# Four graph-attention layers on 32 graphs: value products of two key blocks placed side by side on TensorE, one ring for masked scores and probabilities, a maxima pass that writes its own bank, and moved planned times

## The chip, the cores and the metric

One core of a Trainium2 chip runs the whole program; nothing is shared with other cores. The metric is the device time of one execution in microseconds (us). The kernel before took 2973.89 us in the median of 3 runs (2971.31 to 2974.82).

## What is computed

The input is 32 graphs of 512 nodes with 256 features each (float32) and one 512x512 adjacency matrix that all graphs share. Each graph goes through four residual layers with a layer norm behind each. All four are masked softmax attentions over the 512 nodes:

```python
# layer 0: one head, scores from two vectors
h = x @ W;  e = leaky_relu(s1[:, :, None] + s2[:, None, :]);  x = norm(x + elu(softmax(where(adj, e)) @ h))
# layer 1: eight heads of 32, scores q k^T, then a feed-forward block with two norms of its own
scores = einsum('fnhd,fmhd->fhnm', q, k) / sqrt(32);  attn = softmax(where(adj, scores));  t = attn @ v
# layer 2: four heads of 64, scores from two vectors per head, as layer 0
# layer 3: one head, e = leaky_relu((x W1) (x W2)^T);  x = norm(x + relu(softmax(where(adj, e)) @ (x W3)))
```

## The kernel before

A graph of 512 nodes is four blocks of 128 rows (NB = 4). Products run on PE (TensorE) mostly as float16 high and low parts, accumulated in the eight PSUM banks (`bank_ps`, 128x512 float32 each). Six graphs are in work at a time, in different layers, so that the engines always have something to do.

**The two ways of attention.** Layers 0, 2 and 3 work in units of one head and one block of 128 queries. ACT writes the leaky scores into a bank (`re`, L1115 and L1122; in layer 3 PE makes the scores first, `sc`, L1608). DVE adds the mask, negates and takes the row minimum (`mk`, L1334) into a buffer of the ring `masked` (4 entries). ACT takes the exponential (`ex`, L1133) from there into a buffer of the ring `prob` (7 entries). DVE makes the float16 high part and the row sum (`hi_v`, L1385), POOL the low part (`lo`, L910), a DMA transposes both (`tr`, L856), and PE multiplies them with the values (`pv`, L1627).

Layer 1 takes another way. PE makes the query-key products of four heads at once (`sq`, L1561, four banks), and DVE only needs the largest of each row of them (`mx`, L1349): the full result of that pass goes to a buffer `unused` that nobody reads, of two halves in turn, and each pass waits for the one two before it. The maxima are turned, stored as rows (`mh`, `mt`, `mr`, `md`) and added into the transposed scores. Those are made per pair of heads j (0 to 3), key block kb (0 to 3) and head e of the pair (0, 1): `u` (L1578 and L1579, two matmuls into one bank), ACT's exponential into a `prob` entry (`ue`, L1154), and then `pw` (L1587), once per j and kb: it multiplies the two heads' probabilities, in float32, with `value_ones`, into one accumulating bank (`acc1`), head 0 on its rows 0 to 63 and head 1 on rows 64 to 96. There are 32 x 4 x 4 = 512 `pw`. After kb = 3, `oc` (L1162) copies the bank and `bt` (L1597) turns it back.

**What sets the order.** A host-side planner, `schedule()`, plays the work through as a list schedule: each task has an engine, a planned duration (STEP), tasks that it comes after, ring entries that it opens and closes, and a due time (LEAD x graph + place in the graph's list + LATER of its kind). At each moment an idle engine takes the ready task with the earliest due time. The result is one fixed order for each of PE, ACT, DVE, POOL and SP (the queue that issues all DMAs), and for each ring entry the one who had it before (`prior`), which the code turns into semaphore waits. Each engine works strictly in its order. The `stack` task of SP (L825) is 12 DMA issues that copy q and k into the tensor `stack` of which there is only one: it waits for the last `u` of the graph before. PE's `job` tasks (L1525, L1532) are the dense layers; those of layer 2 (`h2`) wait for transposed rows that SP issues (`xd`, L844).

```python
                elif kind == "pw":
                    j, kb = key
                    pe.wait_ge(*dense_hi.last((g, "v", n) for n in range(2)))
                    bank = bank_of("acc1", g, j) if kb == 0 else bank_ps[entry("bank", "acc1", g, j)]
                    for e in range(2):
                        pe.wait_ge(*exp_done.at(g, j, kb, e))
```

## Time and profile before

| | |
|---|---|
| median of 3 runs | 2973.89 us (2971.31 to 2974.82) |
| the profiled execution: its time, its span | 2974.13 us, 2972.3 us |
| PE busy | 2773.1 us, 93% of the span |
| ACT busy | 2659.7 us, 89% |
| DVE busy | 2560.7 us, 86% |
| POOL busy | 2345.3 us, 79% |
| mean granted TensorE clock | 0.981 |

The time of an execution is its span plus about 2 us around it. Busy time of an engine is the union of its instructions' spans. A group of instructions is told as line, engine, operation, names, shapes and count, then its busy time, the mean duration of one in ns, and the engine's idle time just before them with what ended it. PEld is PE's weight load, which has rows of its own.

### The profile page before, as it was taken

What the parts mean: (1) busy time and instruction counts of PE and PEld (TensorE: products, weight loads), DVE (VectorE), ACT (ScalarE), POOL (GpSimd) and SP (SyncE); (2) the same over time, 40 slices, a digit from 0 to 9 for tenths busy, and PEclk for the clock granted to TensorE, in tenths of its full rate; (3) what the DMA queues carried; (4) which work ended last, traced back from release to release, by engine and by line L of the source; (5) the groups of instructions that cost most, each with busy time, mean ns of one, the idle gap of its engine ahead of it and who ended that gap; (6) DMA issues with size and microseconds to landing.
All of it is one profiled execution on the core that took longest, in us unless ns stands there. A gap on an engine that the chain in (4) does not pass through costs nothing. (4 is left out here: it accounts for less than half of the span.)

```text
span 2972.3 us, 69732 instructions
## 1 busy us (share of the span) xinstructions
PE 2773.1 (93%) x22576; PEld 1510.7 (51%) x22576; DVE 2560.7 (86%) x8261; ACT 2659.7 (89%) x5079; POOL 2345.3 (79%) x2517
## 2 busy tenths in 40 slices
PE   5999999999999999999999999999999999999855
PEld 4444445555555555545555554555555455554433
DVE  6778889889989888998989999898998889889764
ACT  6668889899999999999999999999989999898974
POOL 5467779788878888887888888788887888887774
PEclk9999999999999999999999999999999999999978
DMA  7355567767767767776676767677777777676565
GB/s 172 71 99 107 104 118 133 140 118 143 136 133 127 139 131 135 128 140 129 129 143 129 139 131 135 123 137 133 136 129 136 130 134 140 125 129 118 108 114 100
DMA packets 1215804, 378.91 MB, mean 127 GB/s; under 512 B 1157712, under 2 KB 1194320, under 8 KB 1215440
## 3 DMA queue, kind: packets, MB, share of 16 engines
q1 hardware_dynamic: 1213616, 373.46, 67.6%
q8 instruction: 180, 2.95, 0.4%
q10 hardware_dynamic: 1824, 0.99, 0.2%
q14 instruction: 184, 1.51, 0.2%
HBM read 21.43 MB, written 16.78 MB: 13 GB/s over the span
## 5 line engine op out<-in xcount | busy, mean ns | idle before, releaser
L910 POOL TENSOR_TENSOR split_r<-prob_r,split_r 128x512 f16<-128x512 f32 x768 | 880.5, 1159 | 275.8 <-DVE split_r L1385 272.9
L1349 DVE CUSTOM_DVE_ANT_0 unused<-bank_ps,neg_mask 128x512 bf16<-128x512 f32 x1024 | 661.7, 684 | 121.0 <-PE bank_ps L1561 120.3
L1627 PE MATMUL bank_ps<-val_r,trans_r 128*128 128x64 f16 (+1 forms) x9216 | 631.7, 222 | 72.9 <-DMA trans_r<-split_r 72.2
L1627 PEld LDWEIGHTS bank_ps<-val_r,trans_r 128*128 128x128 f16 x9216 | 526.9, 99 | 252.5 <-DMA trans_r<-split_r 74.8
L1154 ACT ACTIVATE prob_r<-bank_ps 128x512 f32<-128x512 f32 x1024 | 571.6, 607 | 48.7 <-PE bank_ps L1579 43.5
L1133 ACT ACTIVATE prob_r<-masked_r,low_r 128x512 f32<-128x512 f32 x768 | 535.8, 722 | 41.0 <-DVE low_r L1334 35.6
L1385 DVE TENSOR_SCALAR_CACHE_REDUCE split_r<-prob_r 128x512 f16<-128x512 f32 x768 | 510.9, 677 | 49.6 <-ACT prob_r L1133 25.7
L1587 PE MATMUL bank_ps<-prob_r,value_ones 128*33 128x512 f32 (+1 forms) x2048 | 546.1, 611 | 0.1
L1334 DVE CUSTOM_DVE_ANT_0 masked_r<-bank_ps,neg_mask 128x512 f32<-128x512 f32 x768 | 507.9, 683 | 31.0 <-ACT bank_ps L1122 22.9
L1578 PE MATMUL bank_ps<-stack 98*128 98x512 f16 x1024 | 393.3, 384 | 0.4 <-DVE low L1349 0.2
L1579 PE MATMUL bank_ps<-neg_mask_t,identb 128*128 128x512 bf16 x1024 | 389.6, 381 | 0.0
L891 POOL TENSOR_TENSOR split_r<-xcur,split_r 128x512 f16<-128x512 f32 x256 | 291.3, 1158 | 94.3 <-ACT split_r L1002 94.1
L1122 ACT ACTIVATE bank_ps<-spread_r,near 128x512 f32<-128x512 f32 x512 | 340.6, 699 | 14.3 <-DVE low L1349 8.8
L935 POOL TENSOR_TENSOR z<-z,xcur 128x512 f32<-128x512 f32 x192 | 241.7, 1272 | 97.9 <-DVE z L1373 44.0
L1532 PE MATMUL bank_ps<-w_h,xt_r 128*128 128x256 f16 x2304 | 283.0, 276 | 28.9 <-issue 14.7
L1435 DVE BATCH_NORM_STATS2 stats<-z 128x6 f32<-128x256 f32 x768 | 283.4, 415 | 26.1 <-POOL z L935 18.5
L1532 PEld LDWEIGHTS bank_ps<-w_h,xt_r 128*128 128x128 f16 x2304 | 224.4, 99 | 85.7 <-issue 30.0
L1578 PEld LDWEIGHTS bank_ps<-stack 98*128 98x128 f16 x1024 | 99.5, 97 | 275.3 <-issue 96.2
L1197 ACT ACTIVATE z<-z,offset,scale 128x256 f32<-128x256 f32 x384 | 203.4, 595 | 13.6 <-POOL offset L968 13.1
L965 POOL TENSOR_TENSOR scale<-scale,exponent 128x4 f32<-128x4 f32 x192 | 199.1, 1037 | 16.0
L1197 ACT ACTIVATE xcur<-z,offset,scale 128x256 f32<-128x256 f32 x384 | 207.8, 613 | 0.3 <-POOL offset L968 0.3
L1608 PE MATMUL bank_ps<-xt_r,proj_r 128*128 128x512 f16 x768 | 184.5, 382 | 0.0
(148 smaller groups left out, 4532.7 us busy)
## 6 DMA issues: line engine op xcount, KB each, us to landing
stack<-qk SPq DMA_DIRECT2D x384, 128.0 KB, 2.4
xcur<-in_x_dram SPq DMA_DIRECT2D x32, 512.0 KB, 4.0
out_dram<-z SPq DMA_DIRECT2D x32, 512.0 KB, 3.1
trans_r<-split_r SPq DMA_TRANSPOSE x768, 3.3
xt_r<-split_r SPq DMA_TRANSPOSE x320, 3.3
stack<-low_rows SPq DMA_DIRECT2D x128, 4.0 KB
qk<-in_adj_dram SPq DMA_DIRECT2D x1, 1024.0 KB, 7.9
z<-in_L_gnn_W_dram SPq DMA_DIRECT2D x4, 256.0 KB, 12.3
```

The lines of the kernel that those rows point to most:

```text
L910: nc.gpsimd.tensor_tensor(split_r[:, j, 1, :], prob_r[:, i, :], split_r[:, j, 0, :], ALU.subtract).then_inc(lo_done.sem, 1)
L1133: nc.scalar.activation(prob_r[:, entry("prob", *unit), :], masked_r[:, i, :], ACT.Exp, bias=low_r[:, i:i + 1], scale=-1.0).then_inc(probs_ ...
L1154: nc.scalar.activation(prob_r[:, entry("prob", "pt", g, *key), :], bank_ps[entry("bank", "u", g, *key)][:], ACT.Exp).then_inc(exp_done.sem, 1)
L1197: ins = nc.scalar.activation(dst[:, b, :], src[:, b, :], ACT.Identity, bias=offset[s][:, b:b + 1], scale=scale[s][:, b:b + 1])
L1334: nc.vector.tensor_tensor_reduce(out=masked_r[:, i, :], in0=bank_ps[entry("bank", "sc", *unit)][:], in1=neg_mask[:, b, :], scale=-1.0, sca ...
L1349: nc.vector.tensor_tensor_reduce(out=unused[:, nth % 2, :], in0=bank_ps[entry("bank", "sq", g, t, b, h)][:], in1=neg_mask[:, b, :], scale= ...
L1385: nc.vector.tensor_scalar(split_r[:, entry("split", *unit), 0, :], prob_r[:, entry("prob", *unit), :], 1.0, None, ALU.mult, ALU.add, accum ...
L1532: ins = nc.tensor.matmul(bank[:, half * C:(half + 1) * C], turned[:, t, xp, b * P:(b + 1) * P], W[job][:, wp, t, :], start=(i == 0), stop= ...
L1578: nc.tensor.matmul(bank[:], stack[:, h, 1, t, kb * P:(kb + 1) * P], stack[:, h, 0, t, :], start=True, stop=False)
L1579: nc.tensor.matmul(bank[:], identb[:], neg_mask_t[:, kb, :], start=False, stop=True).then_inc(turned_done.sem, 1)
L1587: ins = nc.tensor.matmul(bank[top:(64 if e == 0 else PAIR_COLS), :], value_ones[:, kb, j, cols], prob_r[:, entry("prob", "pt", g, j, kb, e ...
L1627: ins = nc.tensor.matmul(bank[:, at:at + width], trans_r[:, i, pp, jb, :], val(g, layer)[:, vp, jb, cols], start=(n == 0), stop=(n == len( ...
```

## The change

Five things change; what is computed stays the same.

1. `schedule()` runs as before, with the old ring sizes, but returns the planned start of each task. A new function `settle()` moves each planned start by NUDGE (per kind) and OFFSET (per place in the graph's list, 0 to 491), sorts each engine's tasks by the moved starts, and gives out all ring entries anew in that order.
2. For `pw`, the planned starts of kb 0 and 1 are both set to the later of the two, and so are those of kb 2 and 3 (PW_RUN = 2); the OFFSET of each is added behind that.
3. The rings `masked` and `prob` become one of 12 entries. `mk` writes into the entry, `ex` works in place in it. What `ex` waited for (the entry's former user) `mk` on DVE now waits for.
4. `mx` writes its full result into the bank that it reads, and its wait for the `mx` two before is gone; so is the buffer `unused`.
5. FIRST, LAST, SHIFT, LATER, STEP and the planner's rings stay as they are.

NUDGE has 105 entries from -3.4 to 6.8, OFFSET has 357; the places of `pw` in a graph's list are 136, 141, 146, 151 (j = 0), 160, 165, 170, 175 (j = 1), 184, 189, 194, 199 (j = 2) and 208, 213, 218, 223 (j = 3), and that of `stack` is 79. `pw` has no entry in NUDGE.

```diff
+    IN_RING = {"masked": "prob"}
+    RINGS = {**POOLS, "prob": 12}
...
+             "q_lo": 1.7, "rc_0": -0.9, "rc_2": -0.2, "rc_3": -0.6, "re_3": -0.9, "rp": 0.1, "rs_0": 2.9, "rs_1": 3.1, "rs_3":
+             4.9, "rs_ffn": -0.8, "rs_out": 0.1, "sc_3": 0.6, "shift": 2, "skip": 0.7, "spread_0": 0.3, "spread_2": 0.1, "sq":
+             -0.1, "st_0": -0.5, "st_2": 0.4, "st_3": 0.4, "st_out": 0.3, "stack": 6.8, "store": 1.2, "tr_0": -0.3, "tr_2": 0.2,
+             "tr_3": 0.2, "u": -0.2, "x_hi_0": 1.8, "x_hi_1": -1, "x_hi_2": -1.8, "x_hi_3": -1.3, "x_hi_ffn": -0.2, "x_lo_0":
...
+              0.5, 31: 0.2, 32: -0.1, 33: -1, 34: -0.4, 35: 0.7, 36: 1.3, 39: -0.4, 40: -1.4, 42: 1.6, 43: 0.5, 44: -0.3, 47:
...
+              -1.7, 66: 0.1, 67: 0.1, 69: 2.3, 70: -0.5, 71: 1.8, 72: -0.6, 74: -0.7, 75: 1.8, 76: 1.1, 77: -0.6, 79: 2.5, 81:
...
+              131: 2.8, 132: 0.3, 133: 0.1, 135: 1.1, 137: -1.1, 138: -1, 139: -1, 140: -0.9, 141: 0.2, 143: -0.2, 144: -0.4,
+              145: -0.1, 146: -1.5, 147: -0.6, 149: 0.5, 150: -0.2, 152: 0.4, 153: -0.1, 156: 0.2, 157: -0.2, 158: 0.4, 159:
+              0.1, 160: -0.3, 162: 0.6, 163: -0.5, 164: -0.4, 167: -0.7, 168: 2.2, 169: 2, 170: 0.1, 171: -1.2, 172: -1, 174:
+              0.1, 175: 0.1, 176: 0.8, 178: 0.3, 180: -0.1, 181: 1, 183: 0.6, 185: -2.2, 186: -0.5, 187: -0.6, 190: -0.1, 191:
+              1.6, 192: -2.2, 193: -2.2, 194: -0.5, 195: -2.1, 196: 0.5, 197: -2, 198: -0.4, 199: -0.5, 201: -0.5, 203: -0.4,
+              204: -0.1, 205: 0.4, 206: -0.5, 207: 0.5, 208: -0.2, 210: 0.4, 211: 0.5, 212: 0.8, 213: 0.1, 214: -0.4, 215: -0.3,
+              216: -0.5, 218: -0.1, 219: -0.4, 221: 0.8, 222: -0.2, 223: 0.4, 224: 0.8, 226: -0.4, 227: -1.3, 228: -1.1, 229:
...
+    DRIFT = {}
+    PW_RUN = 2
...
+    def settle(order, start):
...
+        for key, (_, us, _, _, closes, lands, (_, nth)) in tasks.items():
+            begin, ahead = start[key], 0.0
+            if key[0] == "pw" and PW_RUN > 1:
+                run = [(*key[:3], kb) for kb in range(key[3] // PW_RUN * PW_RUN, key[3] // PW_RUN * PW_RUN + PW_RUN)]
+                begin = max(start[k] for k in run)
+                ahead = 1e-4 * (tasks[run[-1]][6][1] - nth)
+            moved[key] = begin + NUDGE.get(kind_of(key), 0) + OFFSET.get(nth - first[key[1]], 0) + DRIFT.get(key[1], 0) - ahead
...
+        entries = {name: [[-1e18, None, n] for n in range(size)] for name, size in RINGS.items()}
+        in_turn = sorted(tasks, key=lambda key: (moved[key], tasks[key][6][1]))
+        for key in in_turn:
+            for name, opener in tasks[key][3]:
+                name = IN_RING.get(name, name)
+                if (name, opener) in place:
+                    continue
+                entry = min(entries[name], key=lambda e: (e[0], e[2]))
+                place[name, opener], before[name, opener] = entry[2], entry[1]
+                entry[0] = max(moved[k] + tasks[k][1] + tasks[k][5] for k in closers[name, opener])
+                entry[1] = opener
+        return {engine: [key for key in in_turn if tasks[key][0] == engine] for engine in order}, place, before
...
-        unused = sb("unused", [P, 2, N], bf16)
...
-        masked_r = sb("masked_r", [P, POOLS["masked"], N])
-        low_r = sb("low_r", [P, POOLS["masked"]])
-        prob_r = sb("prob_r", [P, POOLS["prob"], N])
+        low_r = sb("low_r", [P, RINGS["prob"]])
+        prob_r = sb("prob_r", [P, RINGS["prob"], N])
...
-                    was = prior("prob", *unit)
-                    if was is not None:
-                        act.wait_ge(*prob_free(was))
                     act.wait_ge(*masked_done.at(*unit))
-                    i = entry("masked", *unit)
-                    nc.scalar.activation(prob_r[:, entry("prob", *unit), :], masked_r[:, i, :], ACT.Exp,
+                    i = entry("prob", *unit)
+                    nc.scalar.activation(prob_r[:, i, :], prob_r[:, i, :], ACT.Exp,
...
-                        dve.wait_ge(*probs_done.at(*was))
+                        dve.wait_ge(*prob_free(was))
...
-                    nth = largest_done.at(g, t, b, h)[1]
-                    if nth > 2:
-                        dve.wait_ge(largest_done.sem, nth - 2)
+                    bank = bank_ps[entry("bank", "sq", g, t, b, h)][:]
                     eng.sem_inc(masking, 1)
-                    nc.vector.tensor_tensor_reduce(out=unused[:, nth % 2, :], in0=bank_ps[entry("bank", "sq", g, t, b, h)][:],
+                    nc.vector.tensor_tensor_reduce(out=bank, in0=bank,
```

## Rows read from the trace of the kernel before

**Rows 1.** The page: its span, and busy time of each engine.
```profile
span 2972.3 us, 69732 instructions
...
PE 2773.1 (93%) x22576; PEld 1510.7 (51%) x22576; DVE 2560.7 (86%) x8261; ACT 2659.7 (89%) x5079; POOL 2345.3 (79%) x2517
```

**Rows 2.** Busy time of each engine from 300 to 2800 us, with granted clock.
```profile
core 0: us, PE busy (x) PEld busy (x) DVE busy (x) ACT busy (x) POOL busy (x), PEclk, DMA share, GB/s
...
300.00:2800.00 2500.00, 2423.78 (x19886) 1311.54 (x19885) 2234.24 (x7265) 2336.19 (x4468) 2047.16 (x2195) 1.00 0.71 131
```

**Rows 3.** PE's own waits from 300 to 2760 us: total, times, longest.
```profile
PE bank_ps L1627 <- DMA trans_r<-split_r: 21.1, 32, 2.0
PE bank_ps L1532 <- issue: 14.7, 16, 2.4
PE bank_ps L1532 <- DMA xt_r<-split_r: 11.5, 7, 2.5
```

**Rows 4.** Timeline of PE around one pw that stands alone: start, duration, instruction.
```profile
1210.34 0.38 PE L1578 MATMUL bank_ps<-stack 98*128 98x512 f16 x1
1210.56 0.38 PE L1579 MATMUL bank_ps<-neg_mask_t,identb 128*128 128x512 bf16 x1
1210.87 1.07 PE L1587 MATMUL bank_ps<-prob_r,value_ones 128*64 128x512 f32 x4
1211.87 0.39 PE L1578 MATMUL bank_ps<-stack 98*128 98x512 f16 x1
```

**Rows 5.** Timeline of PE at the first and the last of 14 adjacent pairs.
```profile
578.15 0.38 PE L1579 MATMUL bank_ps<-neg_mask_t,identb 128*128 128x512 bf16 x1
578.46 1.93 PE L1587 MATMUL bank_ps<-prob_r,value_ones 128*64 128x512 f32 x8
...
2539.76 1.93 PE L1587 MATMUL bank_ps<-prob_r,value_ones 128*64 128x512 f32 x8
2541.62 0.55 PE L1627 MATMUL bank_ps<-val_r,trans_r 128*128 128x64 f16 x13
```

**Rows 6.** Timeline of PE's weight loads, around the lone pw and in a pair.
```profile
1210.34 0.10 PEld L1579 LDWEIGHTS bank_ps<-neg_mask_t,identb 128*128 128x128 bf16 x1
1210.86 0.19 PEld L1587 LDWEIGHTS bank_ps<-prob_r,value_ones 128*64 128x64 f32 x4 [0.43 <-issue]
1211.87 0.10 PEld L1578 LDWEIGHTS bank_ps<-stack 98*128 98x128 f16 x1 [0.81 <-DVE val_r L1310]
...
2540.65 0.16 PEld L1587 LDWEIGHTS bank_ps<-prob_r,value_ones 128*33 128x33 f32 x2 [0.27 <-issue]
```

**Rows 7.** Timeline of PE at the end of graph 14's layer-1 products, and 18 us on.
```profile
1225.04 1.07 PE L1587 MATMUL bank_ps<-prob_r,value_ones 128*64 128x512 f32 x4
1226.05 0.39 PE L1578 MATMUL bank_ps<-stack 98*128 98x512 f16 x1
...
1227.51 1.07 PE L1587 MATMUL bank_ps<-prob_r,value_ones 128*64 128x512 f32 x4
...
1244.67 1.58 PE L1532 MATMUL bank_ps<-w_h,xt_r 128*128 128x256 f16 x13 [1.12 <-DMA xt_r<-split_r]
```

**Rows 8.** Timeline of SP's DMA issues in the same stretch.
```profile
1226.68 7.93 SPq L825 DMA_DIRECT2D stack<-qk  x12
1234.75 4.06 SPq L856 DMA_TRANSPOSE trans_r<-split_r  x3
1238.93 2.66 SPq L844 DMA_TRANSPOSE xt_r<-split_r  x2
```

**Rows 9.** DVE's groups by shape: busy, mean ns, idle before and releaser.
```profile
L1349 DVE CUSTOM_DVE_ANT_0 unused<-bank_ps,neg_mask 128x512 bf16<-128x512 f32 x1024 | 661.7, 684 | 121.0 <-PE bank_ps L1561 120.3
L1399 DVE TENSOR_TENSOR bank_ps<-bank_ps,rinv 128x512 f32<-128x512 f32 x64 | 44.6, 697 | 1.5
```

**Rows 10.** Waits of ACT and DVE on ring entries: total, times, longest.
```profile
ACT prob_r L1133 <- POOL split_r L910: 4.6, 2, 4.2
...
DVE masked_r L1334 <- ACT prob_r L1133: 3.1, 1, 3.1
```

More of the change, by code:

```diff
@@ L122, in graph_layers_kernel @@
     SHIFT = {}
+    NUDGE = {"add_0": 0.7, "add_3": 2.4, "ap_0": -0.5, "ap_1": -0.6, "ap_2": -2.2, "ap_3": 1, "ap_ffn": -0.4, "ap_out": -0.1,
[13 rows of a table added]
+    OFFSET = {0: -5.3, 1: -2.7, 2: 2.5, 3: -0.3, 4: -0.4, 5: 2.3, 6: -0.3, 7: -0.1, 8: -0.1, 9: 0.2, 11: -0.2, 12: -0.6, 14:
[32 rows of a table added]
+    DRIFT = {}
+    PW_RUN = 2
     STEP = {"add_0": 1.22, "add_1": 1.23, "add_3": 1.23, "ap_0": 0.97, "ap_1": 0.99, "ap_2": 0.98, "ap_3": 0.98, "ap_ffn": 0.98,
@@ L369, in schedule @@
         open_entries = {}
+        start = {}
         now, left = 0.0, len(tasks)
@@ L404, in schedule @@
                 order[engine].append(best)
+                start[best] = now
                 end = now + us
@@ L433, in schedule, with kind_of @@
                 now = events[0]
-        return order, place, before, max(ends.values())
-    ORDER, PLACE, BEFORE, LENGTH = schedule()
+        return order, start, max(ends.values())
+    def settle(order, start):
+        def kind_of(key):
+            return f"{key[0]}_{key[2]}" if key[0] in BY_STAGE else key[0]
+        moved, closers = {}, {}
+        for key, (_, us, _, _, closes, lands, (_, nth)) in tasks.items():
[5 more added lines that the diff above has]
+            moved[key] = begin + NUDGE.get(kind_of(key), 0) + OFFSET.get(nth - first[key[1]], 0) + DRIFT.get(key[1], 0) - ahead
+            for name, opener in closes:
+                closers.setdefault((IN_RING.get(name, name), opener), []).append(key)
+        place, before = {}, {}
+        entries = {name: [[-1e18, None, n] for n in range(size)] for name, size in RINGS.items()}
[10 more added lines that the diff above has]
+        return {engine: [key for key in in_turn if tasks[key][0] == engine] for engine in order}, place, before
+    PLANNED, START, LENGTH = schedule()
+    ORDER, PLACE, BEFORE = settle(PLANNED, START)
     print("planned", LENGTH, {e: round(sum(tasks[k][1] for k in ORDER[e])) for e in ORDER})
@@ L1327, in _ @@
                     layer, h, b = key
-                    i = entry("masked", *unit)
-                    was = prior("masked", *unit)
+                    i = entry("prob", *unit)
+                    was = prior("prob", *unit)
                     if was is not None:
-                        dve.wait_ge(*probs_done.at(*was))
+                        dve.wait_ge(*prob_free(was))
                     dve.wait_ge(*leaky_done.at(*unit))
                     eng.sem_inc(masking, 1)
-                    nc.vector.tensor_tensor_reduce(out=masked_r[:, i, :], in0=bank_ps[entry("bank", "sc", *unit)][:],
+                    nc.vector.tensor_tensor_reduce(out=prob_r[:, i, :], in0=bank_ps[entry("bank", "sc", *unit)][:],
                                                    in1=neg_mask[:, b, :],
```

32 rows, old and new, of tables (NUDGE, OFFSET) are left out of this document.

## The prediction

> **What bounds the kernel now.** I read the page first [rows 1]: PE is busy 2773.1 us of a span of 2972.3 us, ACT 2659.7, DVE 2560.7. PE has the most work, but an average over the span does not say that it sets the pace, so the second view is busy time by stretch [rows 2]. From 300 to 2800 us, where the pipeline of graphs runs full, PE is busy 2423.78 of 2500 us, 97%, at a granted clock of 1.00; ACT is at 93%, DVE at 89%, POOL at 82%. There PE is the bound: it is idle for 76 us only, and a microsecond taken from PE's own work comes off the time unless a new wait replaces it. In the two ends together, 472 us, PE is busy for 2773 - 2424 = 349 us and idle for 123; they go by chains of waits, and I leave them at nothing. Third are PE's own waits in the full stretch [rows 3]: 21.1 us for transposed probabilities, and 14.7 + 11.5 = 26.2 us, in 23 waits, at L1532, where the dense layer of layer 2 waits for transposed rows (its "issue" rows stand at the same point of the cycle). Fourth is the timeline of PE at L1587, the instruction that the change moves most.
>
> **Part 1, pw in pairs.** What does one `pw` cost where it stands alone? A float16 matmul of 512 columns is followed by the next after 0.22 us (1210.34 to 1210.56), but 0.31 us pass before `pw` starts (1210.56 to 1210.87), so entering it costs 0.09 us; the next work starts 1.00 us after it (1211.87) [rows 4]. Together 1.09 us, and 2.18 for two. The trace of before already has 14 places where two `pw` happen to stand side by side; the first and the last show one block of eight matmuls of 1.93 us, and the next work starts 1.86 us after its beginning (2539.76 to 2541.62), with 0.31 us of lead again (578.15 to 578.46) [rows 5]. With the entry that is 1.95 us. A pair that comes to stand together saves 2.18 - 1.95 = 0.23 us. Why it does is seen in the weight loads: the load for a lone `pw` starts with it and the load of the work behind it starts only when that work does, after 0.81 us of idle load path, while in the pair of 2539.76 further loads lie under its running matmuls (2540.65) [rows 5, 6]. The pair pays entry and exit once.
>
> The Trainium skill (TensorE: Matmul & The Clock Gate, "What overlaps and what doesn't") says that a weight load overlaps running matmuls only when it goes to another row group. All loads of `pw` use all 128 rows, so by that rule the two would overlap nothing and pairing would give nothing: this part of the sum would be 0. The trace disagrees already in float16, where the load at 1210.34 runs beside a matmul on the same rows [rows 4, 6], and the pair's 1.95 us disagrees again.
>
> How many pairs form? There are 512 `pw`, so 256 runs of two. `settle` gives both the same start, but then adds OFFSET of each one's own place, and where the two differ something else can be sorted between. The differences are: places 141 and 136 0.2, 151 and 146 1.5, 165 and 160 0.3, 175 and 170 none, 189 and 184 none, 199 and 194 none, 213 and 208 0.3, 223 and 218 0.5. The plan of before starts 116 PE tasks per graph, one each 0.8 us, and most before a `pw` are 0.36 us or longer. Adding the diff's moves to the planned starts around them, by hand for graphs 14 and 15, seven of the eight runs stay together and kb 2 and 3 of j = 0 part. That is 7 x 32 = 224, of which 14 exist: 210 x 0.23 = **48 us** less PE work. Bounds: 242 x 0.23 = 56 us if all form, 6 x 32 = 192, less 14, so 178 x 0.23 = 41 us if one more per graph parts. The price of waiting is small: the pair starts where kb 1 or 3 stood, whose exponentials were done by then; kb 0's two entries of the ring are held one `pw` interval longer, some 2 us [rows 7].
>
> **Part 2, what moves past the last u.** PE's last `pw` of kb 2 stands in front of the last `u` of the graph (1225.04, then 1226.05), that of kb 3 behind it (1227.51) [rows 7]. As a pair both stand behind. SP's `stack` issues wait for that last `u`: they start at 1226.68, take 7.93 us, then three transposes and then the two of the rows that layer 2 needs, until 1241.6 [rows 8], and PE waits for these for 1.12 us at 1244.67 [rows 7]. With kb 2 behind the `u`, SP is let go 1.09 us earlier, while PE, with a pair in place of one `pw` behind the `u`, has 1.95 - 1.09 = 0.86 us more to do before it comes to L1532. So the wait should shrink by up to 0.86 us in each of 28 graphs, and the average of it is 26.2 / 28 = 0.94 us [rows 3]. I take **16 us**, two thirds of 24; bounds are nothing (SP is then held by the low parts of POOL instead) and the whole 26.
>
> One move looks as if it did the same and doesn't. `stack` is moved by 6.8 + 2.5 = 9.3 us later. But its planned duration is 9.6 us, so the next task of SP was planned 9.6 us behind it; 9.3 us later it still stands in front of it, and its 12 issues with it. SP's order is nearly that of before, and I count nothing.
>
> **Part 3, the shared ring.** An attention unit held one entry of 4 and then one of 7; now one of 12. The wait for the old user leaves ACT and goes to DVE. On ACT it ended idle time of 4.6 us in all, and the wait of DVE for a masked buffer 3.1 us [rows 10]; with one entry more, and none held twice, I take nothing. But the place of the wait matters: behind a waiting `mk` DVE holds everything that frees banks for PE. This is the third rival. `ex` in place reads and writes the same memory as before: nothing.
>
> **Part 4, mx into its bank.** A pass takes 684 ns with bf16 output to SBUF. The nearest row for bank to bank, the tensor product at L1399, takes 697 ns [rows 9]. So between nothing and 13 ns each, 1024 x 13 = 13 us more on DVE, of 266 us that it is idle in the full stretch [rows 2]; I take 13 us and nothing on the path. The dropped wait (on the `mx` two before, on the same engine in order) was already met and gives nothing.
>
> **Part 5, the other moves.** Most are below one planned task. They can only win from what PE waits for outside part 2: 76 - 26 = 50 us in the full stretch, 21.1 of it on transposes [rows 2, 3]; they can lose through new waits. I count nothing and put half of 21.1 into the lower end.
>
> **What is late next.** The full stretch gets shorter by 64 us x 28/32 = 56. ACT's 2336 us of work then fill 2336 / 2444 = 96%, from 93%: its cover gets thin, and its in-order waits for DVE and PE begin to reach PE's banks. I give back **10 us**, between nothing and 32, half of the gain.
>
> **The sum.** Profiled execution 2974.1 us - 48 - 16 + 10 = 2920 us. It lies within 0.3 us of the median of the runs, so no correction is made: 2920. Its own range is 2903 to 2938. What a measurement of this kernel can tell from no change is about 0.2%, 6 us.
>
> **Rivals.**
>
> ACT takes over (chance 0.17). It is the second engine and half of PE's gain becomes idle time. For it: 93% against 97% [rows 2], and each of its exponentials stands between two other engines. Against: before, ACT's idle time in the full stretch is 164 us, more than twice what is asked of it. Time: 2974 - 32 = 2942, or down to two thirds given back, 2953.
>
> The moves also take away PE's waits (0.15). All 26.2 us at L1532 go and half of the 21.1 at L1627. For it: `pv_0` and `pv_3` are planned 0.5 and 1.0 us later, behind their transposes. Against: nothing in SP's order changes. Time: 2974 - 48 - 26 - 10 = 2890.
>
> DVE is held by the ring (0.04): slower. `mk` waits on DVE for POOL's low part or PE's pair, and `mx`, `mk` and the copies behind it free the banks. For it: the pairs hold entries longer, and POOL ran 82%. Against: [rows 10]. DVE has 2234 us of work and 13 more in 2500; 768 waits of 0.33 us would fill it. From 0.33 us a wait on, DVE decides; at 0.45 us the whole stretch of 672 `mk` gets 2247 + 302 = 2549 us against 2500, and the time is 2974 + 49 = 3023.
>
> Pairs give nothing (0.04): the eight matmuls don't merge, either because others are sorted between them or because the second waits for its exponentials. Only part 2 is left: 2974 - 16 = 2958.
>
> **How the numbers follow.** The forecast has 0.60. I take 2885 to 2953: the low end is all 256 runs (56 us), all 26 and half of 21.1 with nothing given back, 2974 - 93 = 2881, rounded in, the high end ACT's case in full. Left out are both last rivals and tails of the first, under 2 in 10. Faster by over 0.2%: 0.94; within 0.2%: 0.02; slower: 0.04.
>
> **What would show it.** L1587 should stand in blocks of eight matmuls, some 220 of them, each 1.86 us to the next work, and PE's busy time should fall to some 2773 - 48 = 2725 us (the moved order alone doesn't change it). The wait at L1532 for transposed rows should be a third of what it was. L1349 should read 684 to 697 ns. DVE should show waits for POOL's L910 or PE's L1587 in front of L1334 of a few us in all. I am wrong if blocks of four still rule, if PE's busy time falls but its idle time in the full stretch passes 110 us, or if the gain lies in the ends.

## The result and the profile after

The changed kernel takes 2949.09 us in the median of 4 runs (2946.11 to 2951.89), against 2974.36 us for the kernel before on the same chip: a ratio of 0.992 (95% interval 0.9906 to 0.9934), 25 us faster. The forecast was 2920 us, so less than half of the 54 us came. The profiled execution took 2946.11 us.

In the changed kernel the lines stand about 80 further down: `pw` is L1663 (before L1587), `u` L1654 and L1655, `sq` L1637, `bt` L1673, `pv` L1703, the dense products L1601 and L1608, `mx` L1425, `mk` L1412, `hi_v` L1461, `ex` L1211, `ue` L1232, `oc` L1240, POOL's low parts L972 and L991. The page's first part answers to [rows 1]:

```profile
span 2944.1 us, 68944 instructions
PE 2722.2 (92%) x22360; PEld 1541.9 (52%) x22576; DVE 2589.7 (88%) x8261; ACT 2654.3 (90%) x5079; POOL 2349.9 (80%) x2517
```

PE's 22360 matmul records stand beside 22576 weight loads; before there were 22576 of both. The missing 216 are all of L1655 (x808 of 1024), at 0.22 us each at most 48 us. Where a record is missing, that of the matmul before it covers a part of the hole, so PE's true busy time lies between 2722 and 2770 us, and this page can't judge the term "2725". The trace of `start_fix` can, the changed kernel with four casts in another order (see the experiments), which has all 22576 records:

```profile
PE 2748.8 (93%) x22576; PEld 1544.3 (52%) x22576; DVE 2590.0 (88%) x8261; ACT 2651.7 (90%) x5079; POOL 2350.6 (80%) x2517
```

and its full stretch:

```profile
300.00:2800.00 2500.00, 2418.98 (x20078) 1354.31 (x20076) 2286.92 (x7350) 2355.92 (x4518) 2080.72 (x2225) 1.00 0.71 132
```

So PE's busy time fell by 24 us, not by 48, and PE is idle for 81 us of the full stretch, where it was idle for 76. The size of a pair itself is seen in the timeline of PE, of the changed kernel between 1302 and 1319 us, beside [rows 4, 5].

```profile
1302.27 0.51 PE L1703 MATMUL bank_ps<-val_r,trans_r 128*128 128x64 f16 x12
1302.71 1.93 PE L1663 MATMUL bank_ps<-prob_r,value_ones 128*64 128x512 f32 x8
1304.57 0.87 PE L1703 MATMUL bank_ps<-val_r,trans_r 128*128 128x64 f16 x24
...
1316.34 0.38 PE L1655 MATMUL bank_ps<-neg_mask_t,identb 128*128 128x512 bf16 x1
1316.65 1.93 PE L1663 MATMUL bank_ps<-prob_r,value_ones 128*64 128x512 f32 x8
1318.52 0.39 PE L1637 MATMUL bank_ps<-qk 32*128 32x512 f16 x4
```

Blocks of eight rule: the trace holds 222 of them, one of sixteen and 64 lone blocks of four, and a block of eight gives way to the next work after 1.86 to 1.87 us in most cases (1302.71 to 1304.57, 1316.65 to 1318.52). That is the pair as forecast, in number and in size. Both findings hold together, because busy time is not only work: the record of a 512-column float16 matmul is 0.38 us long, though the next can start after 0.22 us, so a wait of up to 0.16 us behind it is counted as busy. Where each matmul counts with the distance that is usual between it and its next, by the kinds before and behind, PE's work falls by 45 us in `start_fix`, and what lies above it within the busy time grows from 70 to 91. About half of the pairs' saving came back as such short waits. Next the busy time by stretch, with the columns of [rows 2]:

```profile
0.00:300.00 300.00, 238.20 (x1680) 131.63 (x1696) 216.91 (x653) 210.03 (x409) 179.62 (x196) 0.93 0.53 109
300.00:2800.00 2500.00, 2398.72 (x19905) 1354.56 (x20105) 2288.87 (x7349) 2357.68 (x4517) 2080.61 (x2225) 1.00 0.71 132
2800.00:2944.00 144.00, 85.32 (x778) 55.67 (x776) 83.95 (x262) 86.56 (x155) 89.66 (x99) 0.81 0.56 108
```

ACT works for 2357.68 us of the full stretch (before 2336.19) and DVE for 2288.87 (2234.24). PE stays the busiest engine, with 97% in `start_fix` against ACT's 94%. PE's records leave 101 us open here, 20 us of it by the missing records (81 in `start_fix`). PE's own waits there, as in [rows 3] (us in total, times, longest):

```profile
PE bank_ps L1703 <- DMA trans_r<-split_r: 13.8, 24, 1.3
PE bank_ps L1608 <- issue: 12.5, 14, 2.0
PE bank_ps L1637 <- ACT prob_r L1232: 5.5, 17, 0.9
PE bank_ps L1673 <- ACT spread_r L1188: 5.0, 11, 0.5
PE bank_ps L1591 <- DVE low L1425: 4.3, 12, 0.4
```

L1608 waits 12.5 + 2.5 us (the second for transposed rows), where it waited 26.2: 11 us less, of 16 forecast. New are short waits of `sq`, `bt` and the product that makes layer 0's score columns (L1591), 15 us together.

**Where the gain lies in time.** The start of DVE's subtraction that makes the low parts of the maxima (`mh`, L1360 before), the first of each graph, serves as a mark; I take graphs 5 and 29, counted from 0. Before: 457.4 and 2563.9 us, 87.77 us for each of the 24 graphs between. After: 465.7 and 2544.6, 86.62 us. So the start lost 8.3 us, the 24 graphs gave 27.6, and what is left from graph 29 to the end fell from 408.4 to 399.5. In every graph the change gives 1.15 us; the forecast's 54 us over 32 graphs are 1.69.

**The start.** ACT's timeline around 33 us, after:

```profile
32.39 0.61 ACT L1072 CAST w_g<-qk 128x512 f16<-128x512 f32 x1
32.91 1.65 ACT L1083 CAST split_r<-xcur 128x512 f16<-128x512 f32 x3
44.57 0.62 ACT L1083 CAST split_r<-xcur 128x512 f16<-128x512 f32 x1 [10.01 <-DMA xcur<-in_x_dram]
```

and POOL's in the same stretch:

```profile
22.65 2.27 POOL L972 TENSOR_TENSOR split_r<-xcur,split_r 128x512 f16<-128x512 f32 x2 [9.31 <-ACT split_r L1083]
33.60 1.16 POOL L972 TENSOR_TENSOR split_r<-xcur,split_r 128x512 f16<-128x512 f32 x1 [8.68 <-ACT split_r L1083]
34.71 1.15 POOL L979 TENSOR_TENSOR w_h<-xcur,w_h 128x512 f16<-128x512 f32 x1
```

POOL stands still for 8.68 us in front of its fourth low part (the first was made at 12.18 us), where before all four were done and the low parts of the weights began at 24.64 us. The code explains it: the high casts of graphs 0 and 1 are issued ahead of the weight casts in a fixed order, but the semaphore count that POOL waits for is taken from the sorted order, and the moves of `x_hi` put a cast of graph 2 ahead of the last of these four. So POOL waits for a fifth cast, which stands behind all weight casts (32.91). PE's first product with the weights starts at 35.92 us instead of 30.79.

### The profile page after: what moved, and what is told of

Same layout as the page of the kernel before. It is cut to its first block and busy times, and to the rows that moved or that the text cites. A ratio compares the mean times of both kernels' runs of the same rounds, so it can differ in the third digit from the quotient of the medians.

```text
span 2944.1 us, 68944 instructions
## 1 busy us (share of the span) xinstructions
PE 2722.2 (92%) x22360; PEld 1541.9 (52%) x22576; DVE 2589.7 (88%) x8261; ACT 2654.3 (90%) x5079; POOL 2349.9 (80%) x2517
## 5 line engine op out<-in xcount | busy, mean ns | idle before, releaser
L991 POOL TENSOR_TENSOR split_r<-prob_r,split_r 128x512 f16<-128x512 f32 x768 | 882.3, 1160 | 255.1 <-DVE split_r L1461 251.3
L1425 DVE CUSTOM_DVE_ANT_0 bank_ps<-bank_ps,neg_mask 128x512 f32<-128x512 f32 x1024 | 687.2, 712 | 64.5 <-PE bank_ps L1637 64.1
L1703 PE MATMUL bank_ps<-val_r,trans_r 128*128 128x64 f16 (+1 forms) x9216 | 624.0, 221 | 60.0 <-DMA trans_r<-split_r 56.8
L1703 PEld LDWEIGHTS bank_ps<-val_r,trans_r 128*128 128x128 f16 x9216 | 523.5, 98 | 246.6 <-issue 81.3
L1232 ACT ACTIVATE prob_r<-bank_ps 128x512 f32<-128x512 f32 x1024 | 591.4, 625 | 31.9 <-PE bank_ps L1655 27.2
L1211 ACT ACTIVATE prob_r<-prob_r,low_r 128x512 f32<-128x512 f32 x768 | 536.0, 727 | 25.4 <-DVE low_r L1412 24.9
L1461 DVE TENSOR_SCALAR_CACHE_REDUCE split_r<-prob_r 128x512 f16<-128x512 f32 x768 | 513.6, 679 | 51.0 <-ACT prob_r L1211 36.3
L1412 DVE CUSTOM_DVE_ANT_0 prob_r<-bank_ps,neg_mask 128x512 f32<-128x512 f32 x768 | 507.3, 685 | 33.2 <-ACT bank_ps L1203 13.9
L1663 PE MATMUL bank_ps<-prob_r,value_ones 128*33 128x512 f32 (+1 forms) x2048 | 501.9, 603 | 10.0 <-ACT prob_r L1232 1.1
L1654 PE MATMUL bank_ps<-stack 98*128 98x512 f16 x1024 | 392.1, 383 | 12.0 <-DVE low_r L1412 1.9
L972 POOL TENSOR_TENSOR split_r<-xcur,split_r 128x512 f16<-128x512 f32 x256 | 292.5, 1158 | 100.5 <-ACT split_r L1083 99.8
L1655 PE MATMUL bank_ps<-neg_mask_t,identb 128*128 128x512 bf16 x808 | 306.9, 380 | 0.0
L1608 PE MATMUL bank_ps<-w_h,xt_r 128*128 128x256 f16 x2304 | 283.1, 276 | 23.0 <-issue 12.5
L1608 PEld LDWEIGHTS bank_ps<-w_h,xt_r 128*128 128x128 f16 x2304 | 222.0, 99 | 71.5 <-issue 22.1
L1663 PEld LDWEIGHTS bank_ps<-prob_r,value_ones 128*33 128x33 f32 (+1 forms) x2048 | 125.6, 123 | 224.7 <-issue 180.4
L1275 ACT ACTIVATE z<-z,offset,scale 128x256 f32<-128x256 f32 x384 | 212.1, 628 | 11.3 <-POOL offset L1049 11.2
L1654 PEld LDWEIGHTS bank_ps<-stack 98*128 98x128 f16 x1024 | 99.5, 97 | 213.8 <-ACT prob_r L1232 50.5
## 6 DMA issues: line engine op xcount, KB each, us to landing
z<-in_L_gnn_W_dram SPq DMA_DIRECT2D x4, 256.0 KB, 12.5
```

The lines of the kernel that those rows point to most:

```text
L991: nc.gpsimd.tensor_tensor(split_r[:, j, 1, :], prob_r[:, i, :], split_r[:, j, 0, :], ALU.subtract).then_inc(lo_done.sem, 1)
L1211: nc.scalar.activation(prob_r[:, i, :], prob_r[:, i, :], ACT.Exp, bias=low_r[:, i:i + 1], scale=-1.0).then_inc(probs_done.sem, 1)
L1232: nc.scalar.activation(prob_r[:, entry("prob", "pt", g, *key), :], bank_ps[entry("bank", "u", g, *key)][:], ACT.Exp).then_inc(exp_done.sem, 1)
L1275: ins = nc.scalar.activation(dst[:, b, :], src[:, b, :], ACT.Identity, bias=offset[s][:, b:b + 1], scale=scale[s][:, b:b + 1])
L1412: nc.vector.tensor_tensor_reduce(out=prob_r[:, i, :], in0=bank_ps[entry("bank", "sc", *unit)][:], in1=neg_mask[:, b, :], scale=-1.0, scala ...
L1425: nc.vector.tensor_tensor_reduce(out=bank, in0=bank, in1=neg_mask[:, b, :], scale=-LOW_SCALE, scalar=LOW_LIMIT, op0=ALU.add, op1=ALU.min, ...
```

## The experiments

**The start alone.** First only the order of the four early casts was put right:

```diff
+        for n, (g, half) in enumerate(((0, 0), (0, 1), (1, 0), (1, 1))):
+            moved["x_hi", g, 0, half] = n - 1000.0
```

> The changed kernel with one edit: the four first casts of graphs 0 and 1 (x_hi) keep their order at the head of ACT's list, so that the counts that POOL waits for are those of before. Theory start: POOL's low rows of graph 1 then end their wait at 22 us instead of 33.6 us, SP's loads of graphs 4 and 5 go out at 31 us instead of 40.3 us, and the whole run is 9 to 10 us shorter: 2940 us. Rival: the delay at the start is made up for while the pipeline fills, since PE catches up; then 2949 us.

Measured: 2939.22 us (2935.97 to 2946.66), ratio 0.9898 (0.9881 to 0.9914). POOL's w_h starts at 24.24 us again and PE's product at 30.32. So the late start comes from a count, not from an order. What it costs in the end is less sure than the two medians (2949.09 and 2939.22, 10 us apart) make it look. They come from two chips; against the kernel before on its own chip the gain went from 25 to 32 us, 7 us more, and the two intervals just overlap. At the mark of graph 5 the repaired kernel is 3.3 us earlier, at that of graph 29 4.0 us. The repair is worth some 4 to 10 us.

**The pairs alone.** The kernel before, with `settle()` and PW_RUN = 2, no moves, the old rings and the old `mx`. Of the engines' orders only PE's differs from before, and all 256 pairs stand together. `settle()` also gives the ring entries out anew by that order: 622 PSUM banks and 703 `prob` entries have another former user than before.

```diff
-    ORDER, PLACE, BEFORE, LENGTH = schedule()
+    NUDGE, OFFSET, DRIFT, PW_RUN = {}, {}, {}, 2
+    PLANNED, START, LENGTH = schedule()
+    ORDER, PLACE, BEFORE = settle(PLANNED, START)
```

> The kernel before with PW_RUN = 2 and nothing else: no moves, old rings, mx to its own buffer. Only PE's order changes; all 256 runs stand together. Theory pairs pay in full: 242 x 0.23 = 56 us less PE work, 16 less at L1532 (the last u stands ahead of the pair), 10 given back: 2912 us. Rival ACT and DVE take over: at most half arrives, 2940 to 2950 us.

Measured: 3033.88 us, ratio 1.0215 (1.0194 to 1.0235). The sign is the other one. From mark to mark a graph takes 89.54 us (before 87.77), and PE is busy for 2355.70 us of the full stretch's 2500, idle for 144 where it was idle for 76. But waits sprang up on three engines (ACT's groups, last column: idle before, and what ended it; then waits between 300 and 2760 us):

```profile
L1192 ACT ACTIVATE prob_r<-bank_ps 128x512 f32<-128x512 f32 x1024 | 575.4, 610 | 52.0 <-PE bank_ps L1617 24.0 <-PE bank_ps L1625 15.2 <-POOL split_r L948 7.2
L1200 ACT COPY prob_r<-bank_ps 97x512 f32<-97x512 f32 x128 | 74.9, 585 | 59.5 <-PE bank_ps L1625 59.4
```

```profile
PE bank_ps L1599 <- ACT prob_r L1192: 32.2, 30, 2.5
DVE pair_inv L1404 <- PE bank_ps L1635: 28.1, 41, 3.9
DVE masked_r L1372 <- ACT bank_ps L1160: 23.1, 24, 3.5
```

(Here `pw` is L1625, `oc` L1200, `ue` L1192, `sq` L1599, `bt` L1635.) ACT's `oc` waits 59.4 us for the last `pw`, 17.1 before; `sq` waits on PE for ACT's exponentials in 30 places, and the entry that the first block of a pair holds longer costs `ue` 15.2 us (before 1.0). A pair begins where its second block stood and so ends one block, 0.9 us, later than the plan had it. Behind that end stands `oc` in ACT's order, behind `oc` the exponentials, and behind these PE's next `u` and `sq`.

**Which pairs.** `settle()` with pairs for kb 0 and 1 only, then for kb 2 and 3 only (one condition, `key[3] // PW_RUN == 0` or `== 1`).

> The kernel before with only kb 0 and 1 paired (142 pairs stand together, 128 new). Theory oc: what costs in pairs_only is that kb 3's product ends a matmul pair later than planned, and oc waits for it on ACT in front of everything else; kb 0 and 1 have no oc behind them, so their pairs pay: 128 x 0.23 = 29 us less, 2942 us. Rival ring and banks: a pair holds probabilities longer and sends PE to its u too early whichever blocks it joins; then half of the loss of pairs_only, 3000 us.

> The kernel before with only kb 2 and 3 paired (128 pairs). Theory oc: all of the loss is here, ACT waits for L1587 in front of oc some 60 us in all as in pairs_only, and the time is 3020 us or more. Rival ring and banks: half of the loss, 3000 us.

Measured: 2982.6 us (ratio 1.0043, 1.0026 to 1.0061) for the first, 3031.98 (1.0208, 1.0188 to 1.0228) for the last, whose `oc` waits 56.1 us against 17.6. Both expectations for the first missed (2942 and 3000). The loss is in the pairs of kb 2 and 3, whose end `oc` waits for. It isn't in the banks given out anew: the first kernel has the same 622 of them and loses 10 us, the last has 4 and loses 60. Nor is it in `settle()`: the ring kernel below goes through it without pairs and takes 2971.63 us.

**Moving the followers.** Can the lateness be dodged? Once the four followers were planned 1 us later, once `oc` was put one place later on ACT alone (126 of 128), once every pair was planned 0.9 us earlier.

```diff
-    NUDGE = {}
+    NUDGE = {'oc': 1.0, 'bt': 1.0, 'rp': 1.0, 'dp': 1.0}    # first
+    turn[at:at + 2] = turn[at + 1], key                     # second, for each oc in ORDER["act"]
+    NUDGE = {'pw': -0.9}                                    # third
```

> pairs_only with oc, bt, rp and dp planned 1.0 us later (NUDGE), the time that the pair ends later. Theory oc: ACT's wait before oc falls from 59 us to some 15 us and most of the loss goes: 2985 us or less. Rival: the wait is an effect and not the cause, another wait takes its place and the time stays within 10 us of 3034.

> pairs_only with oc one place later in ACT's order, changed with the task behind it in 126 of 128 places; nothing else moves (in pairs_oc_later four kinds were moved on three engines). Theory oc holds ACT: the task behind oc, mostly another exponential, no longer waits for kb 3's product, ACT's wait before oc falls from 59 us to 20 us or less and the time from 3034 to about 2995 us. Rival: the wait only shows that ACT has nothing better to do (it is not the bound), and the time stays within 8 us of 3034.

> The kernel before with its pairs alone (pairs_only, 3033.9 us), and every pair put 0.9 us earlier in the plan, so that the second block of a pair ends where the plan had it. Theory 'the lateness of a pair's end against the plan costs the 62 us': most of it comes back, since ScalarE's oc and PE's sq no longer wait for it, 2975 to 3000 us, and ScalarE's wait of oc for pw falls from 59 us to under 35. Rival 'the planner has no room on PE ahead of the pair': the wait only moves, from oc waiting for pw to pw waiting for ue or for TensorE's work queued behind it, and the time stays at 3020 us or more.

Measured: 3122.37 us (1.0509, 1.0491 to 1.0528), 3081.69 (1.0368, 1.0349 to 1.0387) and 3143.38 (1.0586, 1.0567 to 1.0605). All three missed. The wait of `oc` does go, to 4.1, 2.9 and 22.6 us, and the time grows all the same, so that `oc` waits is not shown to be what the time is lost by. Other waits grow each time; this is ACT's `ue` and `oc` with the pairs planned earlier:

```profile
L1192 ACT ACTIVATE prob_r<-bank_ps 128x512 f32<-128x512 f32 x1024 | 578.3, 603 | 192.3 <-PE bank_ps L1617 186.0 <-POOL split_r L948 3.0
L1200 ACT COPY prob_r<-bank_ps 97x512 f32<-97x512 f32 x128 | 74.5, 582 | 22.7 <-PE bank_ps L1625 22.6
```

`ue` now waits 186.0 us for `u`, probably because the earlier pair pushes `u` back or itself waits for its exponentials; which of the two isn't shown. My reading of the followers, that each has room to spare, fell.

**Letting the planner plan pairs.** Here the list schedule itself makes both blocks of a pair wait for all four exponentials, with neighbouring due times; 169 neighbours come out.

```diff
+                both = range(kb, kb // 2 * 2 + 2)
-                task(("pw", g, j, kb), 1.03, [("ue", g, j, kb, e) for e in range(2)] + ...
+                task(("pw", g, j, kb), 1.03, [("ue", g, j, k, e) for k in both for e in range(2)] + ...
+    due = tasks[(*key[:3], key[3] + 1)][6]; tasks[key] = (..., (due[0] - 1e-3, tasks[key][6][1]))
```

(STEP of `pw` was set from 1.0 to 0.96 with it.)

> No moves, the rings of the kernel before; the list planner itself counts both blocks' ue as wanted by a pair and gives the two blocks neighbouring due times, so it plans round the pairs instead of having them pulled together after the plan. It gives 169 neighbouring blocks instead of 256. Theory 'any plan that knows of the pairs is enough': under 2965 us, near the change's 2949. Rival 'the plan's order is only good where it was tuned by measured moves': 3000 us or more, with long waits of oc, ue and rp as in pairs_only. I lean to the rival.

Measured: 3267.18 us (1.1002, 1.0984 to 1.1019). PE's `pv` alone waits 118.7 us for transposes in 104 places of the full stretch. That this plan knows of the pairs wasn't enough, but the kernel says little on plans that do. The length that its planner prints is 3057.6 us, against 2817.4 for the plan of before: the list schedule got 240 us longer by the changed due times, before any chip ran it. It is also the only kernel here whose mean granted clock in the full stretch is well below full (0.96, against 0.99 to 1.00).

**The moves.** The changed kernel without its moves, then with those of nine kinds alone (`u`, `ue`, `pw`, `oc`, `bt`, `rp`, `dp`, `sq`, `mx`), then with those of all others alone, then with every move at half its size.

```diff
-    NUDGE = {"add_0": 0.7, "add_3": 2.4, ...}
-    OFFSET = {0: -5.3, 1: -2.7, ...}
+    NUDGE = {}
+    OFFSET = {}
...
-            moved[key] = begin + NUDGE.get(kind_of(key), 0) + OFFSET.get(nth - first[key[1]], 0) + ...
+            moved[key] = begin + 0.5 * (NUDGE.get(kind_of(key), 0) + OFFSET.get(nth - first[key[1]], 0)) + ...
```

> The changed kernel with NUDGE and OFFSET empty: pairs, the ring of 12 and mx into its bank, the order of before otherwise. Theory: the moves cost 10 us at the start and gain little elsewhere, so this is faster than the changed kernel: 2925 us. Rival: the moves carry the gain (they keep the stalls at L1532 small): slower than the changed kernel, 2955 us or more.

> The changed kernel with its moves kept only for the tasks of layer 1's pairs and maxima (u, ue, pw, oc, bt, rp, dp, sq, mx); all others stand where the plan has them. Theory: these moves are what repairs the pairs, 2965 us, of the 69 us between no_moves and the changed kernel. Rival: the gain is spread over all moves, and this is half way, 2985 us.

> The changed kernel with the moved times taken back for u, ue, pw, oc, bt, rp, dp, sq and mx alone; all other tasks keep theirs. The opposite half (moves for those nine kinds alone) took 3043.5 us, without any move 3017.8, with all 2949.1. Theory 'the repair sits in the rest of the moves': 2960 to 2990 us. Rival 'the set works as a whole': 3020 us or more, as with the other half. I expect the rival.

> The changed kernel with every planned move at half its size. No moves: 3017.8 us, all: 2949.1. If the repair grows with the size of the moves (tasks put later or earlier by a tendency that the pairs ask for), half of it gives about 2970 to 2990 us. Rival 'the set is a point found by trial, each move useful only beside the others at full size': 3010 us or more, since half of the moves changes the order at as many places as taking them away. PE's waits as the measure: L1654/L1655 and L1637 together under 100 us in the first case, over 120 in the second.

Measured: 3017.81 us (1.0159, 1.0143 to 1.0175) with none, 3043.46 (1.0246, 1.0229 to 1.0263) with the nine kinds', 2997.19 (1.009, 1.0074 to 1.0106) with the others', 3067.92 (1.0327, 1.0311 to 1.0343) with half of each, and 2949.09 with all. The whole set is worth 69 us; one half of the kinds costs 26, the other gives 21, and half the size costs 50. Neither half of the kinds met its expectation (2965 or 2985 for the nine, 2960 to 2990 or 3020 and more for the others). The gain does not grow with the size of the moves; it belongs to the set as a whole. Two of these kernels also carry the late start: POOL waits for 9.67 us with the others' moves and for 10.46 us with half of all, but not with none or with the nine kinds'. The wait of `oc`, without the moves, then with half of them:

```profile
L1195 ACT COPY prob_r<-bank_ps 97x512 f32<-97x512 f32 x128 | 75.0, 586 | 80.0 <-PE bank_ps L1618 79.8
```

```profile
L1240 ACT COPY prob_r<-bank_ps 97x512 f32<-97x512 f32 x128 | 75.1, 587 | 56.7 <-PE bank_ps L1663 55.5
```

The complete moves with lone blocks weren't tried: with them the engines' orders wait for each other in a circle.

**Is it the pairs, or any departure from the order?** Two last kernels leave the blocks of the kernel before lone. One puts each second and fourth block one place later on PE, and changes no other engine's order. The other adds a fixed irregular shift of up to 0.4 us either way to every planned time, which changes some 420 places of PE's order, 250 of ACT's and 540 of DVE's.

```diff
+            moved[key] += 1.1 if key[0] == "pw" and key[3] % 2 else 0                               # lone_late
+            moved[key] += 0.8 * ((7919 * tasks[key][6][1] + 2 * 104729) % 1009 / 1009 - 0.5)        # before_jitter
```

> The kernel before, its blocks lone as they were (nearly: 35 neighbours instead of 14), but the second and the fourth block of every head pair (kb 1 and 3) one place later in PE's order, 256 blocks; no other engine's order changes. If the lateness of the last block is what costs, this kernel pays it without the pair's saving: the pairs alone took 3033.9 us with some 48 us of PE work saved, so this one takes 3030 to 3080 us, with ScalarE's wait of oc for pw well over the 17 us of before. Rival 'a place later costs nothing, the pairs lose for another reason (the first block kept back, the ring's entries held longer)': 2970 to 2990 us.

> The kernel before with a fixed irregular shift between -0.4 and +0.4 us on every planned time, and nothing else: some 420 places of PE's order, 250 of ScalarE's and 540 of VectorE's come out otherwise. If any departure from the plan's order costs, as half of the moves did (3067.9 us, 50 more than none), this one costs 20 to 60 us: 2995 to 3035 us. Rival 'small irregular shifts do not matter, only a shift of one sort in one direction does': 2970 to 2985 us.

Measured: 3064.87 us (1.0302, 1.0278 to 1.0326) and 3040.82 (1.0222, 1.0195 to 1.0249). ACT's `ue` and `oc` in the first and in the second:

```profile
L1192 ACT ACTIVATE prob_r<-bank_ps 128x512 f32<-128x512 f32 x1024 | 571.0, 607 | 67.0 <-PE bank_ps L1617 43.6 <-remote 18.1 <-PE bank_ps L1625 3.6
L1200 ACT COPY prob_r<-bank_ps 97x512 f32<-97x512 f32 x128 | 75.2, 587 | 109.2 <-PE bank_ps L1625 108.5 <-POOL split_r L948 0.6 <-issue 0.2
```

```profile
L1192 ACT ACTIVATE prob_r<-bank_ps 128x512 f32<-128x512 f32 x1024 | 571.9, 608 | 66.7 <-PE bank_ps L1617 42.7 <-remote 18.4 <-PE bank_ps L1625 1.9
L1200 ACT COPY prob_r<-bank_ps 97x512 f32<-97x512 f32 x128 | 74.4, 581 | 14.6 <-PE bank_ps L1625 14.4
```

The lateness alone costs 90 us, with `oc` waiting 108.5 us. But the irregular places cost 66 us too (a little over the expected 20 to 60), without `oc` waiting any longer than before; this is one set of shifts, no other was tried. Both hold: blocks that end one place late cost time without any pair, and the order of before is one in which even small changes of place cost some 2%.

**The orders replayed on paper.** What a new order costs can be estimated without a chip. Let each task take its planned duration (STEP) and start in its engine's order, 0.15 us (the planner's HOP) after the last task and the last former user of its ring entries that it waits for, and take 0.23 us off for each `pw` that stands behind another. The order of before then takes 2817 us, and the others differ from it by this (estimate, then the measured ratio's share of 2972 us):

| kernel | replayed | measured |
|---|---|---|
| pairs alone | +67 | +64 |
| kb 0 and 1; kb 2 and 3 | +14; +61 | +13; +62 |
| `oc` and three more later; `oc` swapped; pairs early | +144; +114; +145 | +151; +109; +174 |
| the planner's own pairs | +234 | +298 |
| change without moves; nine kinds'; the others'; half of all | +41; +66; +40; +74 | +47; +73; +27; +97 |
| lone late; irregular | +88; +89 | +90; +66 |
| the change | +15 | -24 |

So most of the loss can be read off the orders. The replay also tells where it goes. With the pairs alone, `oc` freed from its wait for `pw` brings back 1 of the 67 us, and all waits for ring entries left out bring back 54 (26 each without the waits for `prob` entries or for banks): a pair that ends late holds its entries longer, and the wait of `oc` is for the most part a sign of it. With the blocks lone and late, freeing `oc` brings back 38 of 88. The replay misses the change by 39 us: of the 69 us that the moves give, the plan's own durations explain 26. All of this is an estimate from the plan, no run.

**Ring and maxima.** The kernel before with one ring of 11 for both, pairs and moves left out; the kernel before with `mx` into its own bank; the changed kernel with `mx` into `unused` again and a ring of 11; and that last with the start put right.

```diff
-    RINGS = {**POOLS, "prob": 12}
+    RINGS = {**POOLS, "prob": 11}
-                    nc.vector.tensor_tensor_reduce(out=bank, in0=bank,
+                    nc.vector.tensor_tensor_reduce(out=unused[:, nth % 2, :], in0=bank_ps[entry("bank", "sq", g, t, b, h)][:],
```

> The kernel before with one ring of 11 for masked scores and probabilities, without moves, pairs or mx in its bank. Theory: the ring alone is worth little without pairs, since ACT waited for an entry for 5 us only: 2970 us within 5. Rival: DVE, which now does the waiting, holds the copies behind it: 2990 us.

> The kernel before with mx writing into its own bank, and nothing else. Theory mx costs: mx behind mx starts 6 to 17 ns later, 6 to 17 us of DVE work, of which PE's waits for its banks pass on a part: 2980 us. Rival: DVE's idle time hides it, 2972 us within 3.

> The changed kernel, but mx writes its result to the buffer unused again, with its wait, and the ring has 11 entries for the room. Theory mx costs: mx after mx starts 609 ns after it instead of 626 ns, 17 us less of DVE work, and PE's waits before u and sq shrink: 2941 us. Rival: DVE's idle time hides it all: 2949 us within 3.

> The changed kernel with both repairs: the four first casts in their old order, and mx to the buffer unused with a ring of 11. Theory: they are independent, 10 us at the start and 6 us over the run, so 2949 - 16 = 2933 us, faster than both kernels. Rival: with the start repaired the mx cost is hidden, 2939 us as start_fix.

Measured: ring 2971.63 us (1.0006, 0.9993 to 1.0018), `mx` into its bank 2974.0 (1.0013, 0.9999 to 1.0027), both nothing that can be told apart; `mx` taken back 2943.41 (0.9912, 0.9897 to 0.9928), whose interval overlaps that of the change; both repairs **2935.76** us (2933.63 to 2940.54), 0.9875 (0.9854 to 0.9896), the lowest median here and 13 us under the change. Its interval overlaps that of the start alone (0.9881 to 0.9914), so what `mx` and the ring of 11 add to that repair is not shown.

## Why the prediction was wrong

**By its steps.** What bounds the kernel: right; PE set the pace before and after. Part 1's number and size: right, 224 pairs in 223 blocks where 224 were forecast, each 1.86 us, so some 48 us less of PE's work by the pairs' size. Its sign "PE's busy time falls to 2725" failed: with all records it is 2748.8, since short waits beside the pairs are counted as busy; kb 2 and 3 of j = 0 are apart in every graph, as worked out from OFFSET. By the rule of the Trainium skill weighed there (TensorE: Matmul & The Clock Gate, "What overlaps and what doesn't") the pair would have gained nothing. The trace disagrees again: 1.86 us for a pair against twice 1.00 for a lone block. Part 2: right in mechanism, 11 us of shorter waits at L1608 instead of 16. Part 3: nothing alone, as forecast (2971.63). Part 4: nothing on the path, as forecast, though DVE's work was mis-sized (below). What is late next: ACT's 96% did not come about; it is at 94%, and `ue` and `oc` wait for PE, not PE for the amount of ACT's work.

**What failed.** Two steps, of opposite sign and each larger than the whole gain. The first is Part 1's "the price of waiting is small". It asked whether the exponentials of a pair are ready in time, and not who waits for its end. With 242 more pairs, 242 x 0.23 = 56 us of work went and the kernel became 62 us slower (3033.88 against the 2972 us or so of before), so the price is about 118 us. The term "some 2 us" for the two entries held longer was named and then priced at nothing; by the replay the ring entries carry most of the loss. The second is Part 5's "I count nothing" for the moves: they give 69 us (3017.81 to 2949.09), though some 4 to 10 of what they could give are lost at the start by the miscount of four casts. Between 3033.88 and 3017.81 lie the ring of 12 and `mx` together, 16 us with the pairs present. No run parts the two; the replay, in which `mx` plays no part, gives the shared ring 26 us, so it is probably the ring. Part 3's "I take nothing" holds without pairs and not with them.

In a chain, each step as it was measured: 2972, pairs 3034, ring and `mx` 3018, moves 2949, start put right 2939, `mx` taken back 2936. The forecast's 54 us contain no term of size 118 or 69; that it came within 29 us is luck, their near cancelling. The last two steps of the chain are within what the runs can't tell apart.

The rival "the moves also take PE's waits" was closest in naming the moves, but its place (the two DMA waits, 36 us) was not where they work. The rival on the slower side, a ring that holds an engine, was nearer than its chance of 0.04: it put the loss on DVE's waits in the changed kernel, where it didn't come, and with the pairs alone waits for entries are most of the loss, by the replay. Its threshold has a slip: 253 us of DVE's spare time over the 672 `mk` of the full stretch is 0.38 us a wait, not 0.33, which takes all 768.

**What stays open.** What gives the change the 39 us that the replay doesn't see, and which few of the moves matter. No kind or size of them was found that carries the gain by itself.

## What to carry to other kernels

Where fixed in-order queues feed each other, price a regrouping by who waits for the end of the group and for the buffers that it holds, not only by when its inputs are ready: blocks that end 0.9 us late cost 118 us here, twice the 56 us of saved matmul time. A replay of the new order with the planned durations and all ring waits gives that price beforehand, 67 us slower where 64 were measured. Before forecasting a change of order, measure how sharp the present order is, with a small irregular shift of everything and with the one delay in question alone; if that costs 2%, the work saved is worth only what the new order lets through. Counts for semaphores must be taken from the order that is issued; the wrong ones held POOL up for 8.68 us here. And a busy time is compared only between traces with all matmul records: the missing 216 made PE look some 27 us less busy (2722 against 2749).

## What the runs showed of the hardware

The maxima pass into its own bank has longer records than the forecast's nearest row let expect, and so has the reading of its accumulator. DVE's groups after, then with the pass into SBUF again (mean ns of one is the second number):

```profile
L1425 DVE CUSTOM_DVE_ANT_0 bank_ps<-bank_ps,neg_mask 128x512 f32<-128x512 f32 x1024 | 687.2, 712 | 64.5 <-PE bank_ps L1637 64.1
L1425 DVE DVE_READ_ACCUMULATOR2_ANT low<- 128x1 f32 x1024 | 147.4, 144 | 0.0
```

```profile
L1428 DVE CUSTOM_DVE_ANT_0 unused<-bank_ps,neg_mask 128x512 bf16<-128x512 f32 x1024 | 662.3, 682 | 67.8 <-PE bank_ps L1640 67.0 <-DVE low L1428 0.3
L1428 DVE DVE_READ_ACCUMULATOR2_ANT low<- 128x1 f32 x1024 | 84.7, 83 | 0.0
```

712 + 144 ns against 682 + 83: 91 ns more by the records, where 13 were forecast. The records overlap, though. From the start of one pass to the start of the next, where they follow each other, the mean is 626 ns against 609 before, 17 us in all (the middle value 617 against 611). Likewise ACT's `ue` reads 625 ns after and 607 ns before, with 478 and 477 ns (middle values) from start to start: the mean duration of a record alone is no measure of what an instruction takes of its engine.
